# Routing of a mixture layer: gates in column tiles, bisection and selection in token chunks

## The reference, cut to what matters

```python
def sinkhorn(gates):
    t = jnp.log(jnp.clip(gates, EPS)) / TEMPERATURE
    def body(t, _):
        t = t - jax.nn.logsumexp(t, axis=-2, keepdims=True)
        t = t - jax.nn.logsumexp(t, axis=-1, keepdims=True)
        return (t, None)
    t, _ = jax.lax.scan(body, t, None, length=SINKHORN_ITERS)   # 8
    return jnp.exp(t)
...
gates = jnp.einsum('bhnd,hde->bhne', x4, gate_w)
cg = sinkhorn(gf)
vals, idx = jax.lax.top_k(jnp.transpose(cg, (0, 2, 1)), m)      # b, n, d, e = 16, 1024, 128, 8; m = n // e = 128
gate_values = (vals > 0.5).astype(x.dtype)
routed = xf[jnp.arange(h)[:, None, None], idx]
outputs = jnp.einsum('hmei,eio->hmeo', routed, experts) * gate_values[..., None]
# combine: add each row to its token, divide by 1 + the number of experts that took the token
```

## Time and profile before

| | us |
|---|---|
| median of 3 runs | 5115.28 (5111.17 to 5116.89) |
| the profiled execution | 5113.58 |
| its span | 5111.9 |
| PE busy | 4240.5 (83%) |
| DVE busy | 2958.9 (58%) |
| ACT busy | 2176.7 (43%) |
| POOL busy | 1824.1 (36%) |
| mean granted TensorE clock | 0.902 of full |

### The profile page before, as it was taken

How to read it: one execution, slowest core, us unless ns; L and a number is a source line. 1 busy time by engine, 2 the same in 40 slices (tenths; PEclk the granted TensorE clock), 3 DMA queues, 4 the chain that set the end, 5 groups by cost and what they waited for, 6 DMA issues and landing times. The chain is left out here.

```text
span 5111.9 us, 75190 instructions
## 1 busy us (share of the span) xinstructions
PE 4240.5 (83%) x23183; PEld 1668.8 (33%) x23183; DVE 2958.9 (58%) x5295; ACT 2176.7 (43%) x4005; POOL 1824.1 (36%) x1334
## 2 busy tenths in 40 slices
PE   5399999846999999999999999958999999566323
PEld 2143433324222222222222222234444444344212
DVE  4787878656877767676767677361000000667563
ACT  3333332245266656565656566643434434413100
POOL 1100000037277767676767677860000000303101
PEclk9699999979699999999999999978999999766655
DMA  1255454348222222222222222010000000213204
GB/s 71 62 120 126 107 134 108 88 180 254 36 31 31 32 32 31 32 33 30 34 30 34 30 34 31 7 67 17 0 0 0 0 0 0 103 50 118 88 0 144
DMA packets 178574, 296.66 MB, mean 58 GB/s; under 512 B 43944, under 2 KB 103342, under 8 KB 175806
## 3 DMA queue, kind: packets, MB, share of 16 engines
q1 hardware_dynamic: 150072, 257.14, 22.4%
q10 hardware_dynamic: 23808, 25.17, 1.4%
q0 software_dynamic: 4368, 10.07, 0.6%
HBM read 94.50 MB, written 69.73 MB: 32 GB/s over the span
## 5 line engine op out<-in xcount | busy, mean ns | idle before, releaser
L1638 DVE TENSOR_REDUCE at_mx<-at_side 128x1 f32<-128x512 f32 x2048 | 1294.0, 682 | 417.4 <-PE at_side L1541 406.4
L1712 ACT ACTIVATE at_P<-at_S 128x512 f32<-128x512 f32 x2048 | 1120.3, 600 | 751.5 <-PE at_S L1573 700.5
L1471 POOL TENSOR_TENSOR at_pairs<-at_P 128x2048 f32<-128x2048 f32 x256 | 1160.0, 4532 | 319.3 <-ACT at_P L1712 298.8
L1573 PE MATMUL at_S<-at_qo,at_ko 99*128 99x512 bf16 x2048 | 785.1, 388 | 76.8 <-ACT at_P L1712 75.8
L1541 PE MATMUL at_side<-at_ko,at_qo 96*128 96x512 bf16 x2048 | 789.5, 398 | 43.9 <-DMA at_ko<-qk 23.1
L1989 ACT ACTIVATE ff_hs<-ff_ph,ff_b 128x512 f32<-128x512 f32 x512 | 351.7, 687 | 523.8 <-PE ff_ph L1959 523.8
L1584 PE MATMUL at_num<-at_P,at_rvt 128*32 128x512 f32 x4096 | 551.4, 611 | 0.0
L1959 PE MATMUL ff_ph<-ffn_Y,ff_w 128*128 (+1 forms) x1024 | 524.2, 594 | 8.7 <-DMA ff_b<-in_b_dram 8.7
L1973 PE MATMUL ff_po<-ff_hs,ff_w2s 128*128 128x512 f32 x1024 | 522.6, 592 | 0.0
L2008 DVE SCALAR_TENSOR_TENSOR X<-ff_po,ffn_b2w,X 128x512 f32 (+1 forms) x32 | 24.0, 750 | 822.4 <-PE ff_po L1973 822.4
L819 DVE SCALAR_TENSOR_TENSOR la_dwq<-la_pad,la_taps,la_dwq 128x1024 f32<-128x1024 f32 x384 | 491.5, 1280 | 11.6
(11 more groups left out here) (414 smaller groups left out, 4607.9 us busy)
## 6 DMA issues: line engine op xcount, KB each, us to landing
la_rep<-la_pad SPq DMA_DIRECT2D x512, 162.8 KB, 3.6
qk<-ap_part SPq DMA_DIRECT2D x32, 768.0 KB, 3.7
at_qo<-qk SPq DMA_DIRECT2D x192, 128.0 KB, 4.7
at_ko<-qk SPq DMA_DIRECT2D x192, 128.0 KB, 7.8
n_ln_xs<-X SPq DMA_DIRECT2D x96, 256.0 KB, 2.3
u<-ap_us SPq DMA_DIRECT2D x32, 320.0 KB, 4.0
X<-in_x_dram SPq DMA_DIRECT2D x4, 2048.0 KB, 22.0
proj<-la_y POOLq DMA_DIRECT2D x32, 256.0 KB, 4.8
```

The costliest lines, as they stand in the source:

```text
L1471: g.tensor_tensor(pairs[i % 2][:, :, :], P[a][:, :, :], P[a + 1][:, :, :], ALU.add).then_inc(pair_done, 1)
L1573: pe.matmul(S[n % RING][:, :], ko[u][:, h, j * C:(j + 1) * C], qo[u][:, h, half * CH:(half + 1) * CH], start=True, stop=True).then_inc(s_r ...
L1638: v.reduce_max(mx[:, n // 2, n % 2:n % 2 + 1], side[bank][:, :], AX.X).then_inc(side_saved, 1)
L1712: a.activation(P[k % SLOTS][:, i, :], S[(4 * k + i) % RING][:, :], ACT.Exp).then_inc(p_ready, 1)
```

## The change

In words: `gw` is one copy of the weights with 32 columns, loaded once, and the four matmuls of a group write 32 rows each of the bank in place of adding up. VectorE saves the gates a second time in expert order (`GE`), for the sum over tokens. The last Sinkhorn instruction writes `cgK`, which eight transposes turn into `cgL`: partition 8s+e, column n is expert e's value for token 1024 s + n (16 chunks by 8 experts). In this layout the threshold is one number per partition; comparison and count are one instruction with a sum (`accum_out`), and one matmul with `same_e` adds over the chunks. The 30 rounds now clear the candidate's bit where it misses. The selection scans rows of 1024 tokens, and finds the token and code of each slot per expert by one-hot matmuls on `rank_b` and `code_b`, a comparison with a sum, and a masked sum. ScalarE copies half of `cgL`, and makes `chosen_b` and `rank_b`.

The diff, cut to its core:

```diff
-        gw = m.sb("gw", [C, 4, C])
+        gw = m.sb("gw", [C, 32])
...
-                for j in range(4):
-                    sp.dma_start(gw[:, j, 32 * j:32 * j + E8], D["gate_w"]).then_inc(g_in, 16)
+                sp.dma_start(gw[:, 0:E8], D["gate_w"]).then_inc(g_in, 16)
...
                     for j in range(4):
-                        done = pe.matmul(pp[u][:, :, :].rearrange("p t e -> p (t e)"), gw[:, j, :],
-                                         Y[:, bass.ds((4 * n + j) * CH, CH)], start=(j == 0), stop=(j == 3))
+                        done = pe.matmul(pp[u][32 * j:32 * j + 32, :], gw[:, :],
+                                         Y[:, bass.ds((4 * n + j) * CH, CH)], start=True, stop=True)
...
+                for k in range(E8):
+                    h, at = k // 4, slice((k % 4) * C, (k % 4 + 1) * C)
+                    done = pe.transpose(cgT[:, h, at], cgK[:, k, :, :].rearrange("p s e -> p (s e)"), K["ident"][:, :])
...
                 with pe.Fori(0, BITS + 1) as i:
                     pe.wait_ge(bisect_vec, i + 1)
-                    for c in range(8):
-                        last = pe.matmul(pcn[:, :, :], oneb[:, :], mask[:, 16 * c:16 * c + 16, :], start=(c == 0), stop=(c == 7))
-                    last.then_inc(bisect_mm, 1)
+                    pe.matmul(pcn[:, 0:1], same_e[:, :], count[:, :], start=True, stop=True).then_inc(bisect_mm, 1)
...
+                for e in range(E8):
+                    if e == 1:
+                        pe.wait_ge(where_read, 1)
+                    if e >= 2:
+                        pe.wait_ge(found_read, e - 1)
+                    for bank, row in ((fr[e % 2], rank_b), (fw[e % 2], code_b)):
+                        for h in range(2):
+                            done = pe.matmul(bank[:, h, :], onehot[:, e, :], row[:, h * CH:(h + 1) * CH], start=True, stop=True)
+                    done.then_inc(found_mm, 1)
...
+                    v.tensor_scalar(GE[:, :, bass.ds(16 * n, 16)].rearrange("p e (j k) -> p e j k", k=4),
+                                    for_e, CLIP, None, ALU.max).then_inc(g_saved, 1)
...
-                        step(v.reduce_sum(part[:, :], tmp[:, :, :].rearrange("p t e -> p e t"), AX.X))
+                        step(v.reduce_sum(part[:, :], tmpE[:, :, :], AX.X))
...
                 for i in range(BITS):
-                    step(v.tensor_single_scalar(cand[:, :], thr[:, :], 1 << (BITS - 1 - i), ALU.bitwise_or))
-                    v.tensor_tensor(mask[:, :, :], cg[:, :, :], bc_e(cand[:, :].bitcast(F32)), ALU.is_ge).then_inc(bisect_vec, 1)
+                    bit = 1 << (BITS - 1 - i)
+                    v.tensor_scalar(junk[:, :], cgL[:, :], cand[:, :].bitcast(F32), None, ALU.is_ge, ALU.add,
+                                    accum_out=count[:, :]).then_inc(bisect_vec, 1)
                     v.wait_ge(bisect_mm, i + 1)
-                    step(v.reduce_sum(cnt[:, :], pcn[:, :, :].rearrange("p t e -> p e t"), AX.X))
-                    step(v.tensor_scalar(bit[:, :], cnt[:, :], float(TOP), float(1 << (BITS - 1 - i)), ALU.is_ge, ALU.mult))
-                    step(v.tensor_tensor(thr[:, :], thr[:, :], bit[:, :], ALU.bitwise_or))
+                    step(v.tensor_scalar(miss[:, :], pcn[:, 0:1], float(TOP), float(bit), ALU.is_lt, ALU.mult))
+                    step(v.tensor_tensor(cand[:, :], cand[:, :], miss[:, :], ALU.bitwise_xor))
+                    if bit > 1:
+                        step(v.tensor_single_scalar(cand[:, :], cand[:, :], bit >> 1, ALU.bitwise_or))
...
+                step(v.tensor_tensor_scan(rank[:, :], tie[:, :], zero_row, 0.0, ALU.add, ALU.add))
...
+                v.tensor_tensor_scan(rank[:, :], chosen[:, :], zero_row, 0.0, ALU.add, ALU.add).then_inc(rank_ready, 1)
+                v.wait_ge(token_mm, 1)
+                v.scalar_tensor_tensor(code_b[:, :], cgL[:, :], 0.5, flat(fr[0]), ALU.is_gt, ALU.mult).then_inc(code_ready, 1)
...
+                step(v.tensor_copy(first[:, :], fr[1][:, 1, 0:1]))
...
+                v.tensor_tensor(onehot[:, :, :], here[:, :].rearrange("p (o n) -> p o n", o=1).to_broadcast([C, E8, C]),
+                                emask[:, :].rearrange("p (e o) -> p e o", o=1).to_broadcast([C, E8, C]), ALU.mult)\
+                 .then_inc(onehot_ready, 1)
...
                 for e in range(E8):
+                    v.wait_ge(found_mm, e + 1)
+                    step(v.tensor_scalar(junk[:, :], flat(fr[e % 2]), local[:, e:e + 1], None, ALU.is_le, ALU.add,
+                                         accum_out=pos[:, e:e + 1]))
+                    if e:
+                        v.wait_ge(found_read, e)
+                    v.scalar_tensor_tensor(junk2[:, :], place[:, :], pos[:, e:e + 1], flat(fw[e % 2]), ALU.is_equal, ALU.mult,
+                                           accum_out=code[:, e:e + 1]).then_inc(found_read, 1)
```

More of the change, by code:

```diff
@@ L2275, in phase_route @@
-        pq = [m.ps(f"pq{h}", [C, 64, E8]) for h in range(2)]
-        pw = [m.ps(f"pw{h}", [C, 64, E8]) for h in range(2)]
-        pr = m.ps("pr", [C, E8])
+        zeros = m.sb("zeros", [C, 16, C])
+        cgK = m.sb("cgK", [C, E8, 16, E8])
+        cgL = m.sb("cgL", [C, N])
+        emask = m.sb("emask", [C, E8])
+        same_e = m.sb("same_e", [C, C])
+        earlier = m.sb("earlier", [C, C])
+        token_sum = m.sb("token_sum", [C, C], BF16)
+        chunk = m.sb("chunk", [C, C])
+        ext = m.sb("ext", [C, 2], BF16)
@@ new lines, in phase_route @@
+        slot, slots = m.sb("slot", [C, 1]), m.sb("slots", [C, C])
+        place = m.sb("place", [C, N])
+        cand = m.sb("cand", [C, 1], mybir.dt.int32)
+        miss = m.sb("miss", [C, 1], mybir.dt.int32)
+        count = m.sb("count", [C, 1])
+        ties = m.sb("ties", [C, 1])
+        need, need_here, first, end = (m.sb(x, [C, 1]) for x in ("need", "need_here", "first", "end"))
+        junk, junk2 = m.sb("junk", [C, N], BF16), m.sb("junk2", [C, N], BF16)
+        chosen = m.sb("chosen", [C, N])
@@ new lines, in phase_route @@
+        tie = m.sb("tie", [C, N])
+        rank = m.sb("rank", [C, N])
+        chosen_b, rank_b, code_b = (m.sb(x, [C, N], BF16) for x in ("chosen_b", "rank_b", "code_b"))
+        here = m.sb("here", [C, C])
+        onehot = m.sb("onehot", [C, E8, C], BF16)
+        where = m.sb("where", [C, E8, 2])
+        local, pos, code, wden = (m.sb(x, [C, E8]) for x in ("local", "pos", "code", "wden"))
+        low = m.sb("low", [C, E8], mybir.dt.int32)
+        high = m.sb("high", [C, E8], mybir.dt.int32)
@@ L2368, in _ @@
+                pe.wait_ge(ties_ready, 1)
+                pe.matmul(fr[1][:, 0, 0:1], earlier[:, :], ties[:, :], start=True, stop=True).then_inc(first_ties, 1)
+                pe.wait_ge(chosen_copied, 1)
                 for h in range(2):
-                    pe.matmul(pp[h][:, :, :], lower[:, :], mask[:, 64 * h:64 * h + 64, :], start=True, stop=True)
-                    last = pe.matmul(pq[h][:, :, :], oneb[:, :], mask[:, 64 * h:64 * h + 64, :], start=True, stop=True)
-                last.then_inc(pe_s, 1)
@@ L2373, in _ @@
[L2373 to L2378, removed]
-                for e in range(E8):
-                    h, at = e // 4, slice((e % 4) * C, (e % 4 + 1) * C)
-                    for bank, source in ((pp, onehot), (pq, upto), (pw, wE)):
-                        last = pe.transpose(flat(bank[h])[:, at], source[:, e, :], K["ident"][:, :])
@@ L2383, in _ @@
-                last.then_inc(pe_s, 1)
-                pe.wait_ge(v_ready, ITERS + 4)
-                for e in range(E8):
-                    last = pe.matmul(flat(found[e // 2])[:, (e % 2) * 2 * C:(e % 2 + 1) * 2 * C], onehotT[:, e, :],
-                                     rows[:, e, :, :], start=True, stop=True)
-                last.then_inc(pe_s, 1)
+                    done = pe.matmul(fr[0][:, h, :], token_sum[:, :], chosen_b[:, h * CH:(h + 1) * CH], start=True, stop=True)
+                done.then_inc(token_mm, 1)
@@ L2403, in save @@
+                step(v.tensor_copy(token_sum[:, :], K["mask8"][:, :]))
+                v.wait_ge(const_ready, 2)
+                step(v.tensor_tensor(chunk[:, :], chunk[:, :], K["mask8"][:, :], ALU.mult))
+                step(v.reduce_sum(first[:, :], chunk[:, :], AX.X))
+                step(v.tensor_scalar(ext[:, 0:1], first[:, :], 1.0 / E8, None, ALU.mult))
                 def save(n, u, last):
                     v.wait_ge(g_tp, n + 1)
+                    gates = pq[u].rearrange("p (k j x) -> p j k x", j=4, x=32)[:, :, :, 0:E8]
@@ L2435, in _ @@
                                             tmp[:, :, :].rearrange("p t e -> p (t e)"), ALU.is_gt, ALU.mult))
-                step(v.tensor_tensor(cg[:, :, :], cg[:, :, :], tmp[:, :, :], ALU.add))
-                step(v.memset(thr[:, :], 0))
+                v.tensor_tensor(cgK[:, :, :, :].rearrange("p k s e -> p s k e"), cg[:, :, :].rearrange("p (s k) e -> p s k e", k=E8),
```

(48 more changed lines are left out.)

165 lines of the change are left out of this document (82 added, 83 removed).

## The result

The changed kernel takes 5043.77 us (median of 4 runs, 5042.33 to 5046.39), the kernel before 5113.23 us over the same comparison: ratio 0.9864, 95% interval 0.9847 to 0.9882. It is 69.5 us faster, where 60.7 were forecast.

A forecast was written before the change was run, and what follows sets the result against it. Routing was taken as bound by one engine at a time, mostly VectorE's chain. Gains 20.8 + 6.1 - 2.9 + 17.6 + 19.1 = 60.7 us gave 5054 us, range 5032 to 5070.

The forecast's parts named there:

- What bounds: Routing phase: one engine works at a time, mostly VectorE's chain, so every microsecond taken off it leaves the total.
- Gates: Routing's gates: four quarter-array matmuls side by side and one load; 1.55 us a group for 3.87, gain 20.8 us.
- rival 2: Gates: TensorE's clock stays at 0.50, 9 us less gain, 5063 us; chance 0.11.
- rival 5: Gates: the array's quarters do not run side by side, 3.4 us a group, total 5074 us; chance 0.03.
- Sinkhorn and layout: Sinkhorn: contiguous reductions in 8 iterations gain 6.1 us; new transposes and copies to the chunk layout lose 2.9 us.
- T: Bisection and selection: comparison with running sum, one element per cycle, put at 1.41 us; bisection round 2.70, gain 17.6.
- rival 1: Summing comparisons in SBUF run at two elements per cycle: 17 us more gain, 5037 us; chance 0.13.
- rival 3: 48 summing instructions run at the scan's two cycles: 51 us, total 5105, about no change; chance 0.05.
- rival 4: Summing instructions slower still, T above 2.67 us, kernel slower; at three cycles 5156 us; chance 0.02.
- Selection: Selection after the bisection: scans 2.29 us each, TensorE hidden behind the experts, 41.9 us for 61.0, gain 19.1 us.
- The range: Whole kernel: 5032 us (rival 1, cheapest read, scans at one cycle) to 5070 us (rival 2, dear read, layout and strides).
- the forecast's own range: Whole kernel: 5046 to 5060 us around the forecast of 5054, chance 0.66.

The follow-up runs named there:

- The early bit alone: Changed kernel with the next candidate bit set while TensorE counts: one total of 5043.07 us, bisection 73.13 us.
- the gates as before: Changed kernel with the old gates again (128-column weights, four matmuls adding up in one bank, four loads): 5066.47 us.
- the bare comparison: Changed kernel with the bisection's comparison and sum split into a comparison and a reduction: one total of 5064.59 us.
- the bf16 count: Changed kernel with count and its matrix in bf16: 5032.65 us; with the early bit too 5028.44, with one wait as well 5026.68.

## Why the prediction was right, and where it was off

- **What bounds.** This was right: in all ten experiments an edit of VectorE's chain, or of TensorE's answer in it, moved its own stage and left the others within 0.2 us. The early bit alone moved it by less than its price, 0.10 for 0.19 us a round.
- **Gates.** The gain was right within 1 us (21.75 for 20.8): a group takes 1.58 us for 1.55, and the clock is low at first. The start came 2.5 us sooner, where 1.7 were forecast. The prediction laid the old start to the four loads; the trace lays it to the wait for GpSimd's constants. With the loads alone the matmuls would have begun 0.74 us sooner, so the single load, with the smaller fill ahead of it, brought 1.78, about as forecast, and the dropped wait the rest. Rivals 2 and 5 fall with the clock of 1.00 from 4757.7 on and with the gates as before.
- **Sinkhorn and layout.** A reduction is 0.76 us shorter, as forecast. The first round's answer took 0.54 us, at a granted clock still at 1.00, the others 0.75. The terms listed for the layout add up to 2.7 us and not to 2.9; 2.42 was measured, and the strided writing of `cgK`, put at 0.2, cost nothing (1.23 us, as without the stride).
- **T.** This is the step that was off, in size: T, the comparison with a sum, was put at 1.22 + 0.06 + 0.13 = 1.41 us. The first two terms fit the measured 1.28 us; the third, the read of the sum, costs nothing beyond it, since the read begins before the summing instruction ends. In the bisection that is 0.12 of the 0.16 us by which a round beat its forecast: from the comparison's start to TensorE's it takes 1.34 us, where the forecast had 1.41 and some 0.05 of its 0.69. The rest is small instructions at 0.19 for 0.20. Among the experts it is 20.2 us (4925.89 to 4946.13) for 23.1, and in the two comparisons ahead 2.5 for 2.9. Together that is some 6.9 of the 10.6 us by which the routing's gain passed the forecast. From the earlier trace rows the length of ScalarE's read was taken, 185 ns, and not its place: there too the read begins before the summing instruction ends, and it adds 0.09 us:

```profile
3455.40 0.26 ACT L1883 ACTIVATE rt_p<-rt_pl,rt_cv 16x11 f32<-16x11 f32 x1 [22.64 <-DVEq L1895]
3455.57 0.18 ACT L1883 ACTIVATION_READ_ACCUMULATOR rt_p<-rt_pl,rt_cv 16x1 f32 x1
```

- **Rivals 1, 3 and 4** fall with T = 1.28: the bare comparison runs at 0.75 us as L2483 did, the sum takes the second element per cycle away, and no summing instruction goes at the scan's pace. The Trainium skill ("VectorE: DVE Perf Modes", § The perf-mode tier table) gives `tensor_scalar` on f32 from SBUF two elements per cycle; the trace agrees for the bare comparison (0.75 us) and not for the one with a sum (1.28 us).
- **Selection.** Its parts were right: scans take 2.29 us, as reckoned from the eight short ones, and TensorE's passes are hidden, worth 2.08 us an expert when they are not (2.5 was put as the bound). TensorE's first answers took 2.3 us in place of 2.9.
- **The range.** The mechanisms were right, but every stage gained somewhat more than forecast, and the sum of it left the forecast's own range. The stated range holds the time because its lower end had been drawn for rival 1, which did not happen; that part was luck.

## What to carry to other kernels

Where one engine works at a time, price its instructions one by one, from rows of the same length and form, and compare stages, not totals: the stages agree to 0.2 us where totals scatter by several. An instruction that compares and sums beats two, though it gives up the faster rate of the bare comparison (1.28 against 0.75 + 0.04 + 1.22). In a loop that goes back and forth between engines, look at the type of a one-column matmul (bf16 took 0.39 us off each round; its rounding must not change the answer), at what may be done while waiting, and at how many waits stand ahead of the instruction that needs the answer.

## What was not expected of the hardware

A second wait ahead of the instruction that takes TensorE's answer costs 0.07 to 0.09 us a round, even though what it waits for is long done (the early instruction ends at 4872.77, the one behind the waits starts at 4873.45; 73.13 against 70.61 us for 29 rounds, and 60.90 against 58.75 with the bf16 count); that removing it gives the time back is shown, where the time passes is not. The read of VectorE's sum lies wholly under the instruction that makes it (1.20 to 1.28 us after its start). And TensorE's answer to one f32 column, 0.63 us from its start at half clock, is mostly its two records, each a weight load and a pass (0.59 us), and not fixed latency: one bf16 record answers in 0.22.
